# A decoder of six layers on one core: the bias and mask row of the second cross-attention added on all partitions, and the front of self-attention in another order

## The reference

```
# self-attention
att = einsum('bhqd,bhkd->bhqk', q, k) * scale      # causal mask, softmax, times v, times Wo
# second cross-attention, 64 keys, one head of 256
q = einsum('bld,ed->ble', query, Wq_w) + Wq_b
k = einsum('bld,ed->ble', key, Wk_w) + Wk_b
aw = einsum('bqd,bkd->bqk', q, k) / sqrt(256) * m
aw = where(m == 0, -1e9, aw)
out = einsum('bqk,bkd->bqd', softmax(aw), value)
```

## Time and profile before

| | |
|---|---|
| three runs | 1308.33 us median, 1306.75 to 1310.15 |
| profiled execution | 1311.99 us, of which the span of the rows is 1309.4 |
| TensorE, VectorE, ScalarE, GpSimd busy | 1156.7, 696.5, 586.9, 470.7 us |
| mean granted clock of TensorE | 0.931 of full speed |
| self-attention: projections, front, loop | to about 31.9 us, to 66.9, from there to about 340 |
| recurrence and second cross-attention | 923 to 1071 us |

### The profile page before, as it was taken

The page is one execution under the profiler, slowest core; times in us unless marked ns, Lnnn a source line. Parts: engine busy times, 40 slices in busy tenths (PEclk is TensorE's granted clock), DMA queues, the critical chain, the costliest instruction groups (busy, mean ns, idle before and its releaser), DMA issues. The chain is left out here.

```text
span 1309.4 us, 23737 instructions
## 1 busy us (share of the span) xinstructions
PE 1156.7 (88%) x7517; PEld 840.1 (64%) x7558; DVE 696.5 (53%) x1882; ACT 586.9 (45%) x1071; POOL 470.7 (36%) x906
## 2 busy tenths in 40 slices
PE   7799898999878867999999999999598967999992
PEld 4344444444344534889999999988355655999961
DVE  4766666766255633522222222257687736554647
ACT  3277777777755643313333333322343222567820
POOL 7355332231432331013333232211332166826556
PEclk9599999999988998999999999999698757999996
DMA  9900200000000007401111111140700013867733
GB/s 345 359 2 9 91 1 1 1 0 1 2 1 1 1 1 271 185 18 40 37 38 37 38 37 38 33 137 1 263 14 1 13 60 129 257 196 235 223 105 121
DMA packets 68127, 109.31 MB, mean 83 GB/s; under 512 B 7345, under 2 KB 54962, under 8 KB 65202
## 3 DMA queue, kind: packets, MB, share of 16 engines
q1 hardware_dynamic: 58130, 80.96, 18.1%
q0 software_dynamic: 9888, 27.01, 6.5%
HBM read 65.61 MB, written 42.34 MB: 82 GB/s over the span
## 5 line engine op out<-in xcount | busy, mean ns | idle before, releaser
L1421 ACT ACTIVATE f_work<-f_bank,f_ub 128x128 f32<-128x128 f32 x312 | 89.2, 368 | 204.1 <-PE f_bank L1743 204.1
L496 ACT ACTIVATE att_PT<-att_ST 128x1024 f32<-128x1024 f32 (+1 forms) x192 | 147.7, 808 | 62.3 <-PE att_ST L634 31.1
L541 DVE CUSTOM_DVE_ANT_0 att_junk<-att_RB,att_causal_q 128x128 f32<-128x128 f32 (+3 forms) x256 | 120.7, 488 | 57.5 <-PE att_RB L616 48.4
L1743 PEld LDWEIGHTS f_bank<-f_work,f_xTf 128*128 128x128 f32 x1248 | 145.3, 192 | 3.9 <-DVE f_work L1543 2.0
L1743 PE MATMUL f_bank<-f_work,f_xTf 128*128 128x128 f32 x1248 | 145.8, 275 | 1.5 <-DVE f_work L1543 1.5
L1752 PE MATMUL f_bank<-wd_down,f_work 128*128 x624 | 141.1, 379 | 0.0
L616 PE MATMUL att_RB<-att_kT,att_qT 96*128 96x512 bf16 (+3 forms) x384 | 119.9, 350 | 21.8 <-DVE att_mx L541 6.6
L1752 PEld LDWEIGHTS f_bank<-wd_down,f_work 128*128 128x128 f32 x624 | 115.5, 190 | 14.1
L1372 POOL DMA_INDIRECT Yd<-f_work,f_inv x39 | 38.5, 987 | 196.3 <-DVE f_work L1562 196.3
L1552 DVE COPY f_xTf<-wu_up 128x1024 f32 x78 | 54.1, 695 | 102.6 <-PE f_bank L1743 94.9
L616 PEld LDWEIGHTS att_RB<-att_kT,att_qT 96*128 96x128 bf16 x384 | 33.8, 98 | 112.8 <-issue 39.5
(11 more groups left out here) (463 smaller groups left out, 2184.6 us busy)
## 6 DMA issues: line engine op xcount, KB each, us to landing
Xd<-g_zero SPq DMA_DIRECT2D x1, 12032.0 KB, 40.8
f_xin<-Xd SPq DMA_DIRECT2D x47, 256.0 KB, 3.4
Yd<-f_yo SPq DMA_DIRECT2D x47, 256.0 KB, 2.5
wu_up<-up_w SPq DMA_DIRECT2D x9, 1024.0 KB, 9.3
wd_down<-down_w SPq DMA_DIRECT2D x9, 1024.0 KB, 18.4
w_all<-w SPq DMA_DIRECT2D x6, 768.0 KB, 10.3
wu_up<-Yd SPq DMA_DIRECT2D x16, 256.0 KB, 5.6
w_all<-w SPq DMA_DIRECT2D x1, 2304.0 KB, 17.7
```

What stands on the lines that cost most here:

```text
L496: act.activation(buf[:, :, 0:w], ST[:, 2 * (k % 2):2 * (k % 2) + 2, 0:w], ACT.Exp, scale=float(HD) ** -0.5).then_inc(exp_done, 1)
L541: dve.tensor_tensor_reduce(junk[:, k % RING, 0:w], RB[:, bank, 0:w], G.causal_q[:, 512 - w:512], 1.0, LOWEST, ALU.add, ALU.max, to).then_i ...
L1421: last = act.activation(hT[:, u % 2, m, :], bank[:, UB + m // 4, (m % 4) * P:(m % 4 + 1) * P], ACT.Gelu, bias=ub[:, ds(e, 1), m])
L1743: mm = pe.matmul(bank[:, UB + n, P * m:P * (m + 1)], staged_up[:, kk, at:at + P], xT[:, u % 2, kk, :], start=(kk == 0), stop=(kk == KD - 1))
```

## The change

In the second cross-attention the bias row is made on all partitions: GpSimd copies the bias `bq` 128 times along the free dimension (`bqs`), the step `bq` multiplies with 128 columns instead of one and waits until GpSimd has set up, and `row` and `hide` have 128 partitions. The product with ones is gone from `s`, with the wait for `row_ready` on TensorE. VectorE adds the row to the scores as it reads them from PSUM and frees the bank, then takes the maximum of the sum, and subtracts it, both in SBUF: three operations where there were two.

In the front of self-attention, the queries of head r+1 (or the keys of group 1) are transposed after the fourth maximum of head r, and `trm` r-1 comes after the eighth instead of after the twelfth. The transposes, all but the first two, get two banks of their own, the first two of `ST` (`SPARE`), and the maxima keep the ring of three. TensorE waits for the projections' banks to be read before it uses these, and ahead of the loop for both spare banks to be free.

```diff
-PROLOGUE = [("trK", -1)]
+PROLOGUE = [("trK", -1), ("trQ", -REP)]
 for _r in range(REP):
-    PROLOGUE += [("trQ", _r or -REP)] + [("mx", 12 * _r + k) for k in range(12)]
+    _head = [("mx", 12 * _r + k) for k in range(12)]
     if _r:
-        PROLOGUE.append(("trm", _r - 1))
-PROLOGUE += [("trK", 0), ("trm", REP - 1), ("trQ", 0)]
+        _head.insert(8, ("trm", _r - 1))
+    _head.insert(4, ("trQ", _r + 1) if _r + 1 < REP else ("trK", 0))
+    PROLOGUE += _head
+PROLOGUE += [("trQ", 0), ("trm", REP - 1)]
...
-RING = 3
+RING, SPARE = 3, 2
...
+class Prologue(Placed):
+    def __init__(self, plan):
+        self.plan, self.base, self.at, self.count = plan, [0] * (RING + SPARE), [], [0] * (RING + SPARE)
+        turns = {"mx": 0, "tr": 0}
+        for n, (what, k) in enumerate(plan):
+            kind = "mx" if what == "mx" or n < 2 else "tr"
+            bank = turns[kind] % RING if kind == "mx" else RING + turns[kind] % SPARE
+            turns[kind] += 1
+            self.count[bank] += 1
+            self.at.append((bank, self.count[bank]))
...
-    RB = ps("RB", [P, RING, 512])
+    RB = ps("RB", [P, RING + 4, 512])
-    ST = ps("ST", [P, 4, 512])
+    ST = RB[:, RING:RING + 4, :]
...
                             project(NT - 2)
                             project(NT - 1)
+                            pe.wait_ge(v_read, RINGP + NT - 2)
...
             pe.wait_ge(v_read, RINGP + NT)
+            for n in range(RING, RING + SPARE):
+                pe.wait_ge(bank_free[n], PRO.count[n])
...
-    hide = sb("hide", [1, K2])
-    row = sb("row", [1, K2])
-    one = sb("one", [1, P])
+    hide = sb("hide", [P, K2])
+    row = sb("row", [P, K2])
+    bqs = sb("bqs", [P, KD, P])
...
-                    pool.tensor_scalar(hide[:, :], m_f[0:1, :], 0.0, -1e9, ALU.is_equal, ALU.mult).then_inc(set_up, 1)
+                    pool.tensor_copy(bqs[:, :, :], bcast(bq[:, :], 2, P))
+                    pool.tensor_scalar(hide[:, :], m_f[:, :], 0.0, -1e9, ALU.is_equal, ALU.mult).then_inc(set_up, 1)
...
-                    ch.link(dve.tensor_reduce(top[:, :], scores, AX_X, ALU.max))
                     if q:
                         dve.wait_ge(exp_done, q)
-                    dve.tensor_tensor(sub[:, :, :], scores, bcast(top[:, :], 2, SK), ALU.subtract).then_inc(free[bank], 1)
+                    else:
+                        dve.wait_ge(row_ready, 1)
+                    part = slice(batch(q) * SK, batch(q) * SK + SK)
+                    dve.tensor_tensor(sub[:, :, :], scores, bcast(row[:, part], 1, J), ALU.add).then_inc(free[bank], 1)
                     drained(dve, step)
-                    dve.sem_inc(sub_ready, 1)
+                    ch.link(dve.tensor_reduce(top[:, :], sub[:, :, :], AX_X, ALU.max))
+                    dve.tensor_tensor(sub[:, :, :], sub[:, :, :], bcast(top[:, :], 2, SK), ALU.subtract).then_inc(sub_ready, 1)
...
-                    dve.tensor_tensor(row[:, :], R[0:1, bank, 0:K2], scale[0:1, :], ALU.mult).then_inc(free[bank], 1)
+                    dve.tensor_tensor(row[:, :], R[:, bank, 0:K2], scale[:, :], ALU.mult).then_inc(free[bank], 1)
...
                 if what == "bq":
+                    pe.wait_ge(set_up, 1)
                     for kk in range(KD):
-                        mm = pe.matmul(R[0:1, bank, 0:K2], bq[:, kk:kk + 1], kT[:, kk, :], start=(kk == 0), stop=(kk == KD - 1))
+                        mm = pe.matmul(R[:, bank, 0:K2], bqs[:, kk, :], kT[:, kk, :], start=(kk == 0), stop=(kk == KD - 1))
...
                         for kk in range(KD):
-                            pe.matmul(to, xT[:, j, kk, :], km[:, kk, b * SK:(b + 1) * SK], start=(kk == 0), stop=False)
-                        mm = pe.matmul(to, one[:, :], row[:, b * SK:(b + 1) * SK], start=False, stop=True)
+                            mm = pe.matmul(to, xT[:, j, kk, :], km[:, kk, b * SK:(b + 1) * SK], start=(kk == 0), stop=(kk == KD - 1))
```

More of the change, by code:

```diff
@@ L219, in looped @@
     return placed
-PRO = Placed(PROLOGUE, [0] * RING)
-MID = Placed(PLAN, PRO.after())
+class Prologue(Placed):
[8 more added lines that the diff above has]
+            self.at.append((bank, self.count[bank]))
+PRO = Prologue(PROLOGUE)
+MID = Placed(PLAN, PRO.after()[:RING])
 SIX = Placed(PLAN_6, MID.after(6))
@@ L228, in iteration @@
 def iteration(i):
-    return looped(PLAN, i, RING, TRANSPOSES + ("mx",), PRO.after())
+    return looped(PLAN, i, RING, TRANSPOSES + ("mx",), PRO.after()[:RING])
 def attention_stage(nc, a, G, y_sb, X):
@@ L274, in attention_stage @@
     rden = [sb(f"rden{p}", [P, 4, REP]) for p in range(2)]
-    RB = ps("RB", [P, RING, 512])
-    RBb = [RB[:, n, :].bitcast(BF16) for n in range(RING)]
-    ST = ps("ST", [P, 4, 512])
+    RB = ps("RB", [P, RING + 4, 512])
+    RBb = [RB[:, n, :].bitcast(BF16) for n in range(RING + SPARE)]
+    ST = RB[:, RING:RING + 4, :]
     OT = ps("OT", [P, 512])
@@ L282, in attention_stage @@
     v_ready, negm_ready = sem("v_ready"), sem("negm_ready")
-    bank_ready = [sem(f"bank_ready{n}") for n in range(RING)]
-    bank_free = [sem(f"bank_free{n}") for n in range(RING)]
+    bank_ready = [sem(f"bank_ready{n}") for n in range(RING + SPARE)]
+    bank_free = [sem(f"bank_free{n}") for n in range(RING + SPARE)]
     row_done = sem("row_done")
@@ L1968, in _ @@
             ch.done(pool.memset(half[:, :], -0.5))
-            pool.memset(one[:, :], 1.0)
             for b in range(B):
@@ L2227, in _ @@
                             drained(pe, ("km", 0, kk))
-                        pe.wait_ge(row_ready, 1)
                     for j in range(J):
```

## The result

The change takes 1303.34 us (median of seven, one of which was disturbed and took 3946.63), the kernel before 1308.33 beside it: a ratio of 0.9953, 95% interval [0.9937, 0.9969]. So it is faster by 0.5%; the medians are 5.0, 7.4 and 6.3 us apart. The profiled execution took 1302.48 us, its span is 1300.2 and its mean clock 0.939.

What follows compares the result with a forecast made beforehand. TensorE, busy 88% of the span, was taken to bound the kernel, engines taking turns in the recurrence. Front +0.2, set-up +1.4 and scores -6.4 gave -4.8 us, from 1308.3 to 1303.5 us; range 1299.5 to 1308.0, the forecast's own 1301.5 to 1305.5.

Steps and rivals of the forecast that it cites:

- front, and what is left of it at the block: Self-attention front: 0.3 us gained on VectorE's waits, loop entry 0.5 later; +0.2 us in all.
- set-up, block to s1: Second cross-attention's set-up, up to the first scores: TensorE's `bq` waits for GpSimd, 1.05 us later; cost taken as +1.4.
- first quarter, s1 to s2: First quarter's scores: TensorE 1.44 us earlier, VectorE's three operations end sooner; gain 1.2 us.
- second, s2 to s3: Second quarter's scores: 1.2 us, or 3.4 if the clock no longer falls; 2.3 taken.
- third, s3 to s4: Third quarter's scores: VectorE 0.46 us longer, but its 1.47 wait for the counts goes; gain 0.9.
- fourth, s4 to end: Fourth quarter's scores: TensorE 2.4 us earlier at the low clock, less 0.46 for VectorE; gain 2.0.
- The waits are spread, not removed: Front: three VectorE waits of 5.96 us become seven smaller ones of 5.7 to 5.9; 0.3 us gain.
- the sum from 41.13 to 42.8: Front, after the fourth maximum: product, eight transposes, next product and VectorE's read, giving a 0.8 us wait, four times.
- Rival 3: Front runs at the high clock: +0.2 becomes -2.5, total -7.5 us, 1300.8 us; chance 0.08.
- my dear case: Set-up: the gap makes TensorE begin again, the clock rises up to 3.1 us later; cost 2.1 us.
- Rival 1: Clock helps twice: no fall in the second quarter, no late rise at set-up; -6.8 us, 1301.5 us; chance 0.20.
- Rival 4: VectorE is the bound: third operation paid in each quarter, 4 x 0.46, nothing got back; +3.5 us, 1311.8; chance 0.10.

Runs made afterwards that it cites:

- e1: Only the self-attention front's edits, on the kernel before: 1316.19 us against 1316.47, ratio 0.9999 [0.9987, 1.0011].
- e6: The changed kernel again, on the chip of some of the parts: 1311.57 us against 1318.99 for the kernel before, ratio 0.9948.
- e2: Only the cross-attention's edits (scores), on the kernel before: 1308.72 us against 1316.47, ratio 0.9934 [0.9917, 0.9950].
- e11: The change with GpSimd's copy of the bias made five times, all ahead of `hide`: 1302.88 us against 1308.68 for the kernel before, ratio 0.9958.
- e5: The kernel before, unchanged, for a second profile: one execution, 1315.90 us, beside a median of 1318.99.
- e8: The kernel before without the products with ones, the row made but not added to the scores: 1311.01 us against 1318.99, ratio 0.9947.
- e10: Repeat of e3, beside the change: 1300.65 us against 1308.68 for the kernel before, ratio 0.9939; the change 1302.39.
- e3: The change with the bias copied first on GpSimd, with its own semaphore: 1307.15 us against 1316.47 for the kernel before, ratio 0.9924.
- e7: The kernel before with ones and bias/mask row on 128 partitions, 127 of them zero: 1311.98 us against 1318.99, ratio 0.9956.
- e9: The changed kernel a third time: 1302.39 us against 1308.68 for the kernel before, ratio 0.9950 [0.9937, 0.9963].
- e12: Repeat of e2 on another chip: 1302.07 us against 1308.68 for the kernel before, ratio 0.9953 [0.9937, 0.9969].
- e4: As e3, with the front's last two transposes taking banks from the ring of three: 1306.63 us against 1316.47 for the kernel before, ratio 0.9926.

## Why the prediction was right

It said 1303.5 us, and the time is 1303.34; faster by more than 0.3%, and it is by 0.47% (0.38% by the medians). The total was better than its terms, and that is in part luck: against the second pair of profiles they miss by 0.2 to 1.0 us, against the first by up to 3.0, in both directions. The sums of the pairs are -8.6 and -3.8, and the medians' -5.0 lies between them, as the kernel before is dear in about half of its executions. By the table, against both profiles of before, with the change's first and second:

| term | forecast | first pair | second pair |
|---|---|---|---|
| front, and what is left of it at the block | +0.2 | +0.7 | +1.2 |
| set-up, block to s1 | +1.4 | +2.2 | +1.9 |
| first quarter, s1 to s2 | -1.2 | -2.8 | -1.8 |
| second, s2 to s3 | -2.3 | -5.3 | -2.9 |
| third, s3 to s4 | -0.9 | -1.2 | -0.1 |
| fourth, s4 to end | -2.0 | -2.3 | -2.2 |
| scores in all | -6.4 | -11.5 | -6.8 |
| sum | -4.8 | -8.6 | -3.8 |

(The front's row is front and loop together: 889.64 - 888.91, and 889.91 - 888.76.)

- **Front.** "The waits are spread, not removed": they are spread, but only 3.6 us of them came back, against 5.7 to 5.9. The wait after the eighth maximum was 0.85, as forecast at 0.9; after the fourth it was 0, 0.20 and twice 0.43, not 0.8. The step that failed is the sum from 41.13 to 42.8. The entry to the loop cost 0.9, not 0.5, by the loop's first weights, but only 0.4 by VectorE's first maximum in the loop (a wait of 5.89 for 5.49). The front alone so ended 1.1 to 1.5 us sooner and the forecast +0.2 at its end was wrong. What brought the front's term near the forecast is something that I hadn't foreseen: the loop starts longer ahead of the clock's rise, and the clock falls once more inside the loop (0.7 and 1.7 us in the change, see e1). It did in all eight profiles with the new front (at 146 to 149, in e6 at 228) and in one of six with the old. The clock rises at 67 to 71 in each; the fall is missing where that was 0.5 to 1.3 us behind VectorE's first maximum of the loop, and there where it was 1.6 to 3.0. The new front brings the loop forward and so moves it from the one to the other. This goes together in 14 profiles; no run moved the loop's start alone, and in e6 the fall came 80 us later than in the rest. Rival 3 (high clock in the front) is out: 0.50 to 69.8. Its -2.5 also left out the 0.5 of the loop's entry; by its own terms it was -2.1.
- **The transposes rule.** The front with its denser order stayed at 0.50 with 23.39 of 29.80 us busy. The Trainium skill (TensorE: Matmul & The Clock Gate, Part 4), by which transposes don't count as busy, is not contradicted by this, nor shown: plain products stood there too.
- **Set-up.** The copy took 0.48 and not 0.6, but `hide` 1.00 and not 0.73, and `bq` began 1.4 us later in the block (15.1 from its start for 13.7) where I had 1.05. The four products of the bias took 1.19 and not 1.01. The clock rose 20.3 us into the block and not 17.2, which is the 3.1 of my dear case, and the total of 2.2 is that case's 2.1. The mechanism holds: VectorE waited 2.86, for 2.66 in the earlier trace rows. I had put too little on the late rise (the same 5.4 us from 937.95 would have it 2.95 later, not 3.1, and the copy at 1.7 us would add 0.5 to the sum by its own halving, not 0.9), which came in four of five profiles with this wait (not in e2; e11 not counted). The Trainium skill (GPSIMD Engine Reference, 1. Specifications) says that GpSimd shares its interfaces to SBUF with VectorE. The 1.7 us that I worked out for the copy on that ground did not come, but the sharing isn't ruled out: in e11 the copies took 0.48 and 0.74 us beside VectorE's work, and 0.40 each once VectorE was done (935.6), and `hide` behind them 0.67. It doesn't explain `hide` at 1.00 in the change for 0.73 before, where VectorE worked all the while; that no run isolates.
- **First and fourth quarter.** The products with ones were mis-sized: 0.36 us at the high clock, where leaving them out saves 0.52 in a tile. I had taken the time from the one's start to the next row's start, and missed that their neighbours' instructions are slower beside them (0.59 to the next row for four, where they take 0.43 alone). VectorE's three operations took 1.26 for a forecast of 1.37. The first pair's -2.8 has a further 1.0 in it, the fall at 984.8 (3.4 us) of the first profile, which stands in its first quarter, not in that of e5 or of the change, and which the forecast passed over. In the last quarter GpSimd became the bound where I said it would, above 2.2, and took 0.3 back.
- **Second quarter.** I took 2.3, halfway between "the clock falls anyway" and "the shorter stretch keeps it up". Against the second pair, -2.9, the halfway was near; against the first, -5.3, even the upper end of 3.4 was low. The fall that it turned on was there in all three profiles with narrow products with ones (before, e5, e1) and in none of the eleven without, and the mean clocks of the other executions agree. So the shorter stretch, or what comes with it, keeps the clock up there; which of the two, no run tells apart. Rival 1's first half holds, its second (no late rise) doesn't.
- **Third quarter.** -1.2 and -0.1 for -0.9: the gain was at the low clock of the first profile; in e5 the wait for the counts was 0.44 and there was little to get, as the bracket in the forecast has it.
- **Rival 4.** VectorE as the bound: its third operation costs at most 0.1 in a quarter (e8), not 0.46, and ahead of the first and the fourth quarter's scores VectorE still waits, 1.04 and 4.62.
- **The base.** I made the sum on the span of one execution and carried it to the median. The scores gave 11.5 against that execution and 6.8 against the next; the forecast agreed with the second.

What stays open: why the clock's fall at 984 comes in some kernels and not in others. It came where the first scores start 24.3 to 24.9 us after the clock's rise at the set-up (eight profiles, though not in e5), and not at 23.4 to 23.7 (four) or 25.4 (e2, where it fell at 975). With it s1 to s2 is 1.7 us longer (e10 against the change), so a gain at the set-up that moves a kernel into that band is mostly lost. This is read off the profiles' times; no run moved that start alone. Open too is why the rise at the set-up comes late in some profiles.

## What to carry to other kernels

Where TensorE's clock keeps changing, a gain of one or two us ahead of a stretch is not a gain at the end until several profiles of both kernels say so: here the front's 1.3 us and most of the set-up's 1.9 to 2.4 (e3, e10) were given back, most of the first 80 us later. Read the kernel before twice, too, since one execution's falls can be worth 4 us. And before work is moved from TensorE to another engine, see whether the product that is in the way is narrow: filling it up with zeros gave most of the gain for one memset.

## What was not expected of the hardware

- A product in 32 bits over one partition, 64 columns, cost 0.52 us at the high clock in the place where the same over 128 partitions cost 0.24 (e7).
- The same code of the last part, from `f_half` to the end, ran in 237.1 to 237.5 us on some chips (before, the change, e9 to e12) and 242.5 to 247.0 on others (e1 to e8). The kernel before took 1308.3 and 1308.7 us on the one kind and 1316.5 and 1319.0 on the other, and the ratios agreed.
- GpSimd's `hide`, 128x128 in each, took 1.00 us in the change, its two repetitions, e2 and e12, 0.73 where the copy of the bias no longer stood right ahead of it (e3, e10, e4), and 0.67 behind five copies (e11). In e3 the cast that then stood behind the copy took 0.73 us, where it takes 0.37 in the change.
